# A selective-scan stage in a six-layer kernel: other steps for the front work, a product on GpSimd and some of the C products on GpSimd

## What is computed

```python
x, res = split(layernorm(x_in) @ W_in)
u = silu(depthwise_conv(x, 4 taps) + b_conv)
delta, B, C = split(layernorm(x_in) @ W_x, [64, 80])
delta = softplus(delta @ W_dt + b_dt)
h[t] = exp(delta[t] * A) * h[t-1] + (delta[t] * u[t]) * B[t]
y = sum over the 16 states n of h[.., n] * C[t, n]   +   u * D
out = (y * silu(res)) @ W_out + b_out
```

## Time and profile before

| what | us |
|---|---|
| median of 3 runs | 1914.01 (1911.65 to 1914.02) |
| profiled execution, its own time | 1911.25 |
| its span, first to last instruction | 1909.4 |
| VectorE busy in the span | 1305.5 (68%) |
| TensorE busy in the span | 1555.5 (81%) |
| from the first to the last scan's end and its product | 586.67, from 936.27 to 1522.94 |
| before it: front of the first sequence, from the barrier | about 890 to 936 |

### The profile page before, as it was taken

The page is one execution under the profiler, slowest core; times in us unless marked ns, Lnnn a source line. Parts: engine busy times, 40 slices in busy tenths (PEclk is TensorE's granted clock), DMA queues, the critical chain, the costliest instruction groups (busy, mean ns, idle before and its releaser), DMA issues. The chain is left out here.

```text
span 1909.4 us, 22713 instructions
## 1 busy us (share of the span) xinstructions
PE 1555.5 (81%) x7774; PEld 1119.2 (59%) x7774; DVE 1305.5 (68%) x3178; ACT 554.5 (29%) x1062; POOL 409.4 (21%) x362
## 2 busy tenths in 40 slices
PE   1676788666599999997678878787887769999998
PEld 1565454555489999985233333333333368999997
DVE  2666666467656666642597987989989865666653
ACT  0000344100012111211464554655545302211211
POOL 1003000000000000000364555655556400000000
PEclk9888899798899999997699898898998979999999
DMA  4000000000000000000000000000000000000000
GB/s 118 1 1 1 1 1 1 1 1 1 1 1 1 1 1 1 1 1 0 1 1 0 1 1 1 1 0 1 1 1 1 0 1 1 7 12 7 7 7 12
DMA packets 12208, 9.15 MB, mean 5 GB/s; under 512 B 2423, under 2 KB 11582, under 8 KB 11966
## 3 DMA queue, kind: packets, MB, share of 16 engines
q1 hardware_dynamic: 12094, 7.70, 1.4%
HBM read 5.60 MB, written 2.10 MB: 4 GB/s over the span
## 5 line engine op out<-in xcount | busy, mean ns | idle before, releaser
L890 PE MATMUL bank<-wqkv_sb,xe 128*128 128x192 f32 x2048 | 380.1, 329 | 0.0
L890 PEld LDWEIGHTS bank<-wqkv_sb,xe 128*128 128x128 f32 x2048 | 353.5, 193 | 17.0 <-DVE xe L1257 0.3
L428 POOL TENSOR_TENSOR rstd<-ve,half_neg 128x4 f32<-128x4 f32 x48 | 48.3, 1007 | 1078.4 <-DVE ve L1081 1078.4
L1007 PE MATMUL bank<-both,ident 128*128 128x512 f32 x512 | 274.1, 630 | 0.0
L1257 DVE TENSOR_TENSOR xe<-xnT,bank 128x512 f32<-128x512 f32 x256 | 175.3, 686 | 105.2 <-PE bank L878 102.5
L660 ACT ACTIVATE bank<-dt,A 128x512 f32<-128x512 f32 x256 | 175.0, 687 | 129.5 <-DVE xe L1319 80.7
L454 POOL TENSOR_TENSOR both<-du,prob 128x512 f32<-128x512 f32 x128 | 162.3, 1269 | 142.8 <-DVE hs L1319 90.3
L454 POOL TENSOR_TENSOR both<-du,prT 128x512 f32<-128x512 f32 x128 | 161.5, 1268 | 80.7 <-DVE xe L1319 45.1
L733 PEld LDWEIGHTS bank<-exp_sb,xe 128*128 128x128 f32 x1024 | 155.2, 224 | 5.0
L1319 DVE TENSOR_TENSOR_SCAN hs<-bank,both 128x512 f32<-128x512 f32 x128 | 155.1, 1212 | 0.0
L1319 DVE TENSOR_TENSOR_SCAN xe<-bank,both 128x512 f32<-128x512 f32 x128 | 155.0, 1211 | 0.0
(11 more groups left out here) (224 smaller groups left out, 2190.0 us busy)
## 6 DMA issues: line engine op xcount, KB each, us to landing
xs<-in_x_dram SPq DMA_DIRECT2D x8, 256.0 KB, 4.4
out_dram<-xs SPq DMA_DIRECT2D x8, 256.0 KB, 2.3
wqkv_sb<-in_wqkv_dram SPq DMA_DIRECT2D x1, 1536.0 KB
exp_sb<-in_expT_dram SPq DMA_DIRECT2D x1, 512.0 KB
wo_sb<-in_wo_dram SPq DMA_DIRECT2D x1, 512.0 KB
win_sb<-in_W_in_dram SPq DMA_DIRECT2D x1, 256.0 KB
wout_sb<-in_W_out_dram SPq DMA_DIRECT2D x1, 128.0 KB
wq_sb<-in_WqT_dram SPq DMA_DIRECT2D x1, 64.0 KB
```

The costliest lines, as they stand in the source:

```text
L890: m = pe.matmul(bank[4 + j // 2][:, (j % 2) * 3 * HD:(j % 2 + 1) * 3 * HD], x_e, wqkv_sb[:, e, :], start=(e == 0 and j % 2 == 0), stop=(e ...
L1007: pe.matmul(bank[4 + k % NH][:], ident[:], hc[k % HRING], start=False, stop=(SUM_RANK[k] == sums_of(k // UNITS, k % NH))).then_inc(hc_used, 1)
```

## The change

The front steps of the scan layer get other ticks and another order: conv0, dlt, bcT, conv1, z0, z1, res0, res1. Both halves of conv0 are now at even ticks before the sequence's first tick (-4, -2), those of conv1 at 8 and 10; every front step of TensorE is at an even tick, behind that tick's spread of C. du moves from VectorE to GpSimd (ticks 17 and 21), without its factor 0.5, which is made up for in D (no longer halved) and in yg (0.25). States 3, 8 and 13 are put in `ON_POOL`: six of 32 products of a sequence are GpSimd's, with three copies of C on ScalarE. The spread of C is at tick 2s for those states too. The activation table loads are placed anew: two for each sequence as before, one more for the first.

```diff
-ON_POOL = ()
+ON_POOL = (3, 8, 13)
-FRONT7 = {"xT": -6, "rows": -4, "conv0": -1, "conv1": 2, "res0": 9, "res1": 12, "bcT": 14, "dlt": 16, "z0": 18, "z1": 22}
+FRONT7 = {"xT": -8, "rows": -6, "conv0": -4, "dlt": 0, "bcT": 2, "conv1": 8, "z0": 12, "z1": 16, "res0": 20, "res1": 22}
-SCAN_CLOCK = range(-UNITS - 10, ALL + 12)
+SCAN_CLOCK = range(-UNITS - 14, ALL + 12)
...
 (GpSimd)
+                    for h in range(NH):
+                        pool.wait_ge(dt_made, seen(NH * b + h + 1))
+                        pool.wait_ge(u_made, seen(NH * b + h + 1))
+                        pool.tensor_tensor(du[b % 2][:, h, :], dt_[b % 2][:, h, :], u2[b % 2][:, h, :], ALU.mult).then_inc(gates_made, 1)
+                        yield
-                steps = on_clock(front, (-8,))
+                steps = on_clock(front, (-12, 17, 21))
...
 (ScalarE, front: order now tanh 0, dlt, bcT, tanh 1, z0, z1, gate tanh 0 and 1)
-                steps = on_clock(front, (-7, -5, 0, 3, 10, 13, 15, 17, 19, 20, 23, 24))
+                steps = on_clock(front, (-10, -7, -1, 1, 3, 11, 13, 14, 17, 18, 21, 23))
...
 (TensorE)
-                steps = on_clock(front, (-6, -4, -1, 0, 2, 3, 9, 12, 14, 16, 18, 22), back, (OUT7,))
+                steps = on_clock(front, (-8, -6, -4, -2, 0, 2, 8, 10, 12, 16, 20, 22), back, (OUT7,))
-                    if 0 <= U < ALL and U % 2 == on_pool(U):
+                    if 0 <= U < ALL and U % 2 == 0:
                         spread_C(U // 2)
...
 (VectorE)
-            link(dve.tensor_scalar(dhalf[:], dhalf[:], 0.5, None, ALU.mult))
-                        dve.wait_ge(dt_made, seen(NH * b + h + 1))
-                        dve.scalar_tensor_tensor(du[par][:, h, :], dt_[par][:, h, :], 0.5, u2[par][:, h, :], ALU.mult, ALU.mult).then_inc(gates_made, 1)
-                        yield
-                        dve.scalar_tensor_tensor(yg[:, h, :], bank[4 + h][:], 0.5, g2[par][:, h, :], ALU.mult, ALU.mult).then_inc(yg_made, 1)
+                        dve.scalar_tensor_tensor(yg[:, h, :], bank[4 + h][:], 0.25, g2[par][:, h, :], ALU.mult, ALU.mult).then_inc(yg_made, 1)
-                steps = on_clock(front, (-9, -7, -3, 1, 4, 11, 14, 21, 22, 25, 26), back, (4, 5, 8))
+                steps = on_clock(front, (-13, -11, -5, 0, 12, 15, 19, 22, 24), back, (4, 5, 8))
```

More of the change, by code:

```diff
@@ L232, in macaron @@
         Dmat = sb("Dmat", [P, NH, P])
-        dhalf = sb("dhalf", [P, NH])
+        D_sb = sb("D_sb", [P, NH])
         A = sb("A", [P, NH, NS])
@@ L352, in macaron @@
             (kc[:], K_conv),
-            (dhalf[:], D.rearrange("(h p) -> p h", p=P)), (A[:], A_log.rearrange("(h p) n -> p h n", p=P)),
+            (D_sb[:], D.rearrange("(h p) -> p h", p=P)), (A[:], A_log.rearrange("(h p) n -> p h n", p=P)),
         ]
@@ L476, in scan_weights @@
                     pool.tensor_tensor(wcv[:, k, :], win_sb[:, 0:DI], tap_rows[k // 2][:, (k % 2) * DI:(k % 2 + 1) * DI], ALU.mult)
-                pool.tensor_tensor(Dmat[:], ident[:].unsqueeze(1).to_broadcast([P, NH, P]), dhalf[:].unsqueeze(2).to_broadcast([P, NH, P]), ALU.mult)
+                pool.tensor_tensor(Dmat[:], ident[:].unsqueeze(1).to_broadcast([P, NH, P]), D_sb[:].unsqueeze(2).to_broadcast([P, NH, P]), ALU.mult)
                 link = chain.link
@@ L613, in front, with tanh_u @@
                     yield
-                    act.preload_act_table_set("exp_and_others")
-                    for h in range(NH):
+                    def tanh_u(h):
                         act.wait_ge(bank7_ps, seen(IN7[f"conv{h}", b]))
                         act.activation(th[:], bank[7][:], ACT.Tanh, scale=0.5).then_inc(th_made, 1)
-                        yield
[L619 to L622, removed]
+                    if b == 0:
+                        act.preload_act_table_set("exp_and_others")
+                    tanh_u(0)
+                    yield
+                    act.wait_ge(bank7_ps, seen(IN7["dlt", b]))
+                    act.activation(dlt[0:DR, :], bank[7][0:DR, :], ACT.Copy).then_inc(dlt_sb, 1)
+                    yield
                     act.wait_ge(bank7_ps, seen(IN7["bcT", b]))
@@ L625, in front @@
                     yield
-                    act.wait_ge(bank7_ps, seen(IN7["dlt", b]))
-                    act.activation(dlt[0:DR, :], bank[7][0:DR, :], ACT.Copy).then_inc(dlt_sb, 1)
+                    tanh_u(1)
                     yield
@@ L638, in front @@
                         act.activation(lz[:], ez[:], ACT.Ln, bias=1.0).then_inc(ln_made, 1)
+                        yield
+                    act.preload_act_table_set("exp_and_others")
+                    for h in range(NH):
+                        act.wait_ge(bank7_ps, seen(IN7[f"res{h}", b]))
+                        act.activation(thr[:], bank[7][:], ACT.Tanh, scale=0.5).then_inc(thr_made, 1)
                         yield
@@ L941, in front, with conv @@
                     yield
-                    for h in range(NH):
+                    def conv(h):
                         into_bank7(f"conv{h}", b)
@@ L950, in front @@
                         yield
[L951 to L954, removed]
+                    yield from conv(0)
+                    into_bank7("dlt", b)
+                    pe.matmul(bank[7][0:DR, :], wx_sb[:, 0:DR], xpad[:, 1:L + 1], start=True, stop=True).then_inc(bank7_ps, 1)
+                    yield
                     pe.wait_ge(bc3_made, seen(b + 1))
@@ L961, in front @@
                     yield
-                    into_bank7("dlt", b)
-                    pe.matmul(bank[7][0:DR, :], wx_sb[:, 0:DR], xpad[:, 1:L + 1], start=True, stop=True).then_inc(bank7_ps, 1)
-                    yield
+                    yield from conv(1)
                     for h in range(NH):
@@ L967, in front @@
                         pe.matmul(bank[7][:], wdt_sb[:, h * P:(h + 1) * P], dlt[:], start=True, stop=True).then_inc(bank7_ps, 1)
+                        yield
+                    for h in range(NH):
+                        into_bank7(f"res{h}", b)
+                        pe.matmul(bank[7][:], win_sb[:, DI + h * P:DI + (h + 1) * P], xpad[:, 1:L + 1], start=True, stop=True).then_inc(bank7_ps, 1)
                         yield
@@ L1275, in front, with u_of @@
                     yield
-                    for h in range(NH):
+                    def u_of(h):
                         dve.wait_ge(th_made, seen(NH * b + h + 1))
@@ L1280, in front @@
                         dve.scalar_tensor_tensor(u2[par][:, h, :], th[:], 1.0, bank[7][:], ALU.add, ALU.mult).then_inc(u_made, 1)
+                    u_of(0)
+                    yield
+                    u_of(1)
+                    yield
+                    for h in range(NH):
+                        dve.wait_ge(ln_made, seen(NH * b + h + 1))
+                        dve.scalar_tensor_tensor(dt_[par][:, h, :], bank[7][:], 0.0, lz[:], ALU.max, ALU.add).then_inc(dt_made, 1)
                         yield
```

## The result

Interleaved with the kernel before, the changed kernel takes 1906.18 us (median of 7, 1905.19 to 1907.73), the kernel before 1913.17: the ratio is 0.9965, 95% interval 0.9953 to 0.9977. It is faster by 7 us, and 1866 with a range of 1842 to 1893 had been predicted. The direction was right and the size was not.

What follows compares the result with a forecast made beforehand. VectorE was taken to set the pace. Savings of 27.8 + 14.8 + 4.4 + 0.5 = 47.5 us took the profiled 1911.25 to 1863.7; with 2.8 for the median, 1866 us, range 1842 to 1893.

Steps and rivals of the forecast that it cites:

- Products and du off VectorE: Scan layer: 48 C products moved to GpSimd save VectorE 27.8 us, du moved there saves 14.8 us.
- a rival: GpSimd and VectorE collide: seven row splits cost 14 us, du's saving loses 7 us; 1887 us, chance 0.04.
- Waits, 67.9 to 63.5 us: VectorE's waits from first scan to last product: 40.6 + 2.9 + 20 = 63.5 us against 67.9, 4.4 us less.
- the burst: Sums held to tick 7, between C(3) and C(4) on TensorE: VectorE waits 5.8 us at product 8, 2.9 in first sequence.
- the rest: Waits outside the burst, from C(1), conv1, ticks 16 to 19, rows and C(0): 20 us, bounds 12 and 40.
- The late sums: GpSimd products' sums come three ticks later on TensorE; those of units 26 and 27 delay C(1) by 0.6 us.
- half rate spreads: Rival: TensorE at half rate in every burst and a late conv step before C(0); 92 us waiting, 1895 us, chance 0.18.
- Around the stretch: Before the first scan, nmr and xn lie beside the gate steps: 0.5 us less, between 2 less and 2 more.
- A sequence of about 71 us: Sign for right: one sequence of 32 units, 76.75 us before, takes about 71 us.
- 4.5 to 7 us at product 8: Sign for right: VectorE's longest wait stands at product 8 and takes 4.5 to 7 us.
- a granted clock under 0.85: Sign for wrong: TensorE's granted clock in the scan layer falls under 0.85.
- a rival of its own: TensorE stays at full rate: bursts of 7.9 us everywhere, 46.4 us of waiting, 1849 us, chance 0.24.

Runs made afterwards that it cites:

- 1891.5: The changed kernel with no state in ON_POOL, so all C products on VectorE, new front steps and du on GpSimd kept: 1891.47 us, ratio 0.9887.
- 1884.9: The changed kernel without fillers, sums of units 0 to 5 spread, conv1 at ticks 16 and 18, z0, z1 and du moved: 1884.86 us, ratio 0.9848.

## Why the prediction was wrong

Of the 47.5 us predicted, 6.1 came in the profiled execution (1911.25 to 1905.19). By its own steps:

- *Products and du off VectorE, 42.6 us.* The counts were right: 208 products on VectorE, 48 on GpSimd at 1.27 us, du at 1.265. VectorE's busy time fell by 34.7. The missing 8 are the collisions in the split (8.1 us), which the C products bring. I had the row for them, called it a rival and priced it at 21 us with a chance of 0.04; the part of it in the row split, 14 us there, happens in every sequence and measures 8. I also read du's mean of 1135 ns without its spread: 672 at its shortest, so most of the 14 already met GpSimd.
- *Waits, 67.9 to 63.5 us.* This is the term that failed: it measures 89.8, 26 us more. It was made of two figures. For the burst I took 9.2 us of TensorE and a wait of 5.8; it is 10.4 and 7.1, and over the layer 52.8 us for 43.5. For the rest I took 2.5 us a sequence, 20 in all; it is 37 in all, and 5.3 in the fourth sequence (0.99, 0.62, 0.68, 0.34, 0.27, 1.82, and smaller ones). The places were partly right: 0.6 at C(1), and a wait before u at half rate was named as a bound. None was counted before product 22.
- *What was wrong in it.* I counted TensorE's work by its amount, tick by tick, at full rate, and let the half rate in only through the range of one place. The late sums were priced where they go (0.6 us for units 26 and 27) and not where they come from. A sum taken out of ticks 18 to 20 and 29 to 30 left TensorE little to do (the first of these places is made longer by VectorE's slower split), and the next step ran at half rate. That rate is what the term missed: with fillers the waits are 52.1 us, with clock 0.99, and without them 89.8, with 0.87. The rival "half rate spreads" had the mechanism, with 1895 us and a chance of 0.18. Its waits were right (92 us for 89.8), but its time was 11 us low, since it had no price for the collisions, and none for what lies outside the stretch.
- *Around the stretch.* Predicted: 0.5 us less. Measured: 6.6 more, of which 3.4 behind the last scan (a wait of 4.16 us before yg, for 0.75). TensorE, at first at half rate behind a wait of 3.3 us, has six sums left there (12 records in 6.90 us; before, four sums, 8 records in 3.60). I had named no price for it.
- *Against the prediction's "what would show it".* "A sequence of about 71 us" is 75.1; "4.5 to 7 us at product 8" is 7.1 with the residual addition just before it and 4.15 without, so it misses by a little on either count; C(3) to C(4) is indeed not under 7.9; "a granted clock under 0.85" was the sign for wrong, and 0.87 was enough. GpSimd never held VectorE up by dB, as forecast.

With the rate held by fillers, the changed kernel takes 1864.7, close to the 1866 that was predicted for it as it stands. That agreement is luck in its parts: VectorE's busy time fell by 36.0 us in that run, not 42.6, and its waits by 15.8, not 4.4. For full rate the prediction had a rival of its own, 1849 us with 46.4 us of waits; the 52.1 measured are 5.7 more, VectorE's work is 6.6 more, and the rest lies outside the stretch. So the count of TensorE's work was near, and the rate was the large part left out.

## What to carry to other kernels

When work is taken off the engine that sets the pace, look at what its consumers on TensorE do meanwhile: a step that comes later leaves a hole where it was, and what stands behind the hole can take twice its time. Look for real work of the same engine to put into the hole (here a convolution), before taking more off the busy engine, and see in the trace if it is enough: here it held the rate beside fillers elsewhere, and by itself only shortened the half rate. Count an engine that falls to half rate by the place of its waits, not by its share of busy time. And when work is moved to GpSimd, look at which operations of VectorE with two operands in SBUF will then run beside it.

## What was not expected of the hardware

- More matmuls made the kernel faster. 42 idle ones in a sequence, some 12 us of TensorE's busy time in the layer, took 41.5 us off.
- A single wait of 2.11 us of TensorE at tick 4 was followed by half rate (1.2 GHz, where 2.4 is full), and so were pairs of waits of 1.4 to 2.8 us with one short matmul between. A wait of 2.44 us at tick 20 was followed by full rate in one run and by half rate in another. A period of 75.08 us held the same three half-rate places for several sequences. In runs with less regular sequences (1891.5, 1884.9) how long the half rate lasts differs from one to the next.
- VectorE's subtraction of two SBUF operands of 128x128 took 1.25 us in six of six sequences where GpSimd had two operations in a row at that place, 0.29 where it had a pause there, and 0.29 beside a busy GpSimd with one operand in PSUM. The Trainium skill (SBUF — State Buffer, the section on the two separate sides) calls the shared port pair an exclusive lock that is held for the whole instruction; the 1.25 us, about one GpSimd operation of 1.27, agree with that, and so does the move of the wait to the next such operation.
